# All experts' weights resident on chip, one VectorE copy per tile, states and layer norm in place, and a reordered step, in a fused attention and mixture-of-experts kernel

## The reference

```python
xn = _layernorm(x, axis=-1)
x = x + attn(xn) + ffn(xn)

# attn: per token, 8 heads of 16 channels
qkv = query @ W_qkv.T + b_qkv
qq, kq, vq = encode(q), encode(k), encode(v)     # unit length, times exp(1j*phase)
q_ent, k_ent = _entangle(qq, g), _entangle(kq, g) # DEPTH = 3 rounds over neighbouring heads
for c in range(CIRCUITS):                        # 4
    pattern = einsum('bsid,bsjd->bsij', conj(qa), ka)
    scores = abs(pattern) ** 2 * SCALING
    amps = sqrt(softmax(scores) + 1e-12)
    ...                                          # weighted values, clipped amplitude, mixed
return measured @ W_out.T + b_out

# ffn: top 2 of 8 experts, hidden size 512
topk_scores, topk_idx = top_k(x_flat @ Wg, 2)
h = gelu(x_flat @ W1[e] + b1[e]); out_e = h @ W2[e] + b2[e]
y = y + cw[:, e:e + 1] * out_e
```

## Time and profile before

| | |
|---|---|
| median of 3 runs | 1484.06 us (1478.45 to 1485.84) |
| the profiled execution, its own time | 1484.62 us |
| its span, first to last instruction | 1482.9 us |
| granted TensorE clock, mean | 0.813 of full speed |
| busy: PE, PEld | 947.4 us (64%), 750.0 us (51%) |
| busy: ACT, DVE, POOL | 740.2, 578.7, 431.4 us |
| DMA | 210.90 MB, 142 GB/s |

### The profile page before, as it was taken

How to read it: one execution, slowest core, us unless ns; L and a number is a source line. 1 busy time by engine, 2 the same in 40 slices (tenths; PEclk the granted TensorE clock), 3 DMA queues, 4 the chain that set the end, 5 groups by cost and what they waited for, 6 DMA issues and landing times.

```text
span 1482.9 us, 28381 instructions
## 1 busy us (share of the span) xinstructions
PE 947.4 (64%) x10529; PEld 750.0 (51%) x10529; DVE 578.7 (39%) x1098; ACT 740.2 (50%) x1602; POOL 431.4 (29%) x389
## 2 busy tenths in 40 slices
PE   3454748487583866858486594848658574866842
PEld 2324547375462746656364464637446463746531
DVE  5541615345160443437152252525425151433421
ACT  3422637365361755727373472836445282655522
POOL 3064101035022130707132040424603021251146
PEclk9865979889796897968798797878978787987965
DMA  7326474755847566695855758485674838576462
GB/s 216 103 82 150 124 148 118 148 158 160 152 135 126 135 146 143 170 173 147 159 133 129 145 149 151 126 178 145 161 159 133 145 106 178 147 151 153 132 103 71
DMA packets 320744, 210.90 MB, mean 142 GB/s; under 512 B 155296, under 2 KB 281952, under 8 KB 320096
## 3 DMA queue, kind: packets, MB, share of 16 engines
q1 hardware_dynamic: 311392, 188.10, 55.9%
q0 software_dynamic: 8192, 16.79, 3.8%
q10 hardware_dynamic: 1024, 4.20, 1.8%
HBM read 147.51 MB, written 61.50 MB: 141 GB/s over the span
## 4 chain that ended last, share of the span: by engine, by line
PE 42%; issue 26%; ACT 17%; POOL 5%; DVE 3%; SPq 3%; DMA 2%; ACTq 1%; POOLq 0%; DVEq 0%
PE ps_h L677 11%; PE ps_f L685 8%; PE ps_a L755 6%; PE ps_r L834 6%; PE ps_k L743 3%; POOL rows_in L1280 3%; ACT hid L1107 2%; PE ps_a L781 2%; ACT L1107 2%; ACT expo L1075 1%; ACT xy L1023 1%; PE ps_f L669 1%; PE ps_f L687 1%; ACT L1075 1%; ACT xy L1045 1%
## 5 line engine op out<-in xcount | busy, mean ns | idle before, releaser
L677 PE MATMUL ps_h<-turned,w_tile 128*128 128x128 f32 x1248 | 216.0, 328 | 334.0 <-issue 235.3
L677 PEld LDWEIGHTS ps_h<-turned,w_tile 128*128 128x128 f32 x1248 | 190.5, 231 | 371.4 <-issue 266.2
L1107 ACT ACTIVATE hid<-ps_h,w_tile 128x128 f32<-128x128 f32 x624 | 178.2, 368 | 340.5 <-PE ps_h L677 336.5
L685 PE MATMUL ps_f<-w_tile,hid 128*128 128x128 f32 x1248 | 198.7, 312 | 0.7 <-ACT turned L1100 0.7
L685 PEld LDWEIGHTS ps_f<-w_tile,hid 128*128 128x128 f32 x1248 | 187.0, 229 | 1.5 <-issue 1.0
L1252 POOL TENSOR_TENSOR sqx<-sqx,sqy 128x512 f32<-128x512 f32 x64 | 82.0, 1303 | 344.4 <-ACT sqy L1031 255.6
L1280 POOL DMA_INDIRECT rows_in<-xn,row_of x128 | 128.3, 1003 | 183.2 <-DVE tile_expert L1637 146.9
L1252 POOL TENSOR_TENSOR v_tok<-qkv,rnorm 128x512 f32<-128x512 f32 x16 | 41.4, 2587 | 395.3 <-DVE rnorm L1533 341.0
L834 PE MATMUL ps_r<-sqx,mats 128*128 128x512 f32 x256 | 132.6, 642 | 17.8 <-POOL sqx L1252 9.6
L1295 POOL DMA_INDIRECT got<-rows_out,row_of x112 | 109.1, 974 | 102.1 <-DMA rows_out<-turned 70.3
L755 PE MATMUL ps_a<-k_rows,q_rows 128*32 128x16 f32 x4096 | 102.2, 245 | 41.6 <-DMA k_rows<-states 29.0
(11 more groups left out here) (249 smaller groups left out, 1566.5 us busy)
## 6 DMA issues: line engine op xcount, KB each, us to landing
w_tile<-w_cat SPq DMA_DIRECT2D x156, 514.0 KB
states<-fxyT SPq DMA_DIRECT2D x32, 512.0 KB, 2.9
k_rows<-states SPq DMA_DIRECT2D x128, 128.0 KB, 5.4
x_tile<-rows_in SPq DMA_DIRECT2D x156, 64.0 KB, 3.1
rows_out<-turned SPq DMA_DIRECT2D x156, 64.0 KB
q_rows<-states SPq DMA_DIRECT2D x128, 64.0 KB, 5.1
rows_in<-v_rows SPq DMA_DIRECT2D x2, 2496.0 KB, 12.0
v_dram<-v_tok SPq DMA_DIRECT2D x16, 256.0 KB, 4.0
```

The source lines that it names most:

```text
L677: last = nc.tensor.matmul(ps_h[:, c, :], w_tile[:, n % WS, c * P:(c + 1) * P], turned[:, x_turn(n) % FS, 0, :], start=True, stop=True)
L685: nc.tensor.matmul(ps_f[:, 1, :], hid[:, n % 2, c, :], w_tile[:, n % WS, HID + c * C:HID + (c + 1) * C], start=(c == 0), stop=False)
L1107: act.activation(hid[:, n % 2, c, :], ps_h[:, c, :], ACT.Gelu, bias=w_tile[:, n % WS, HID + HC * C + c:HID + HC * C + c + 1]).then_inc(hid ...
```

## The change

**Weights.** All eight experts stay on chip: `w_res` holds, per expert, W1 (512 columns), b1 (4) and W2 (512), and `b2_res` the bias b2. `w_cat`, `w_tile`, `b_tile` and `load_weights` are gone. VectorE copies W1 and b1 of a tile's expert (516 columns) from `w_res` to one of three slots of `w_up` (`copy_ups`), and reads the expert into a register first; `tile_up` takes the weights from there. `tile_down` reads W2 and b2 straight from `w_res` and `b2_res` at an address in a register, so TensorE too reads `tile_expert` into a register for every tile.

**Room for that.** The states are grown in place in `xy1` (`fxyT` is gone); the layer norm is done in place in `xn` (`x_sb` is gone), so x is loaded a step later; `sqp`, `mixed`, `power` and `below` lie in `w_rows` and `u`; `got` has one buffer instead of two, so `gather` waits for the sum of the block before (`added_step` of `at - 1`).

**Order.** `pattern(k)` moves from the start of the step to behind the second tile, `grow_once`, `turn_w`, `weighted`, `mix_circuits` and the pieces of ScalarE and VectorE that belong to them move too; on SyncE `load_values`, `store_states` and `load_states` stand at three places instead of two.

```diff
@@ sync @@
-                if exists(ln_block(k + 1)):
-                    load_x(ln_block(k + 1))
+                if exists(ln_block(k)):
+                    load_x(ln_block(k))
...
-                    if at == 6 and exists(n_next):
-                        store_states(n_next)
                     if at == 7 and exists(n_next):
                         load_values(n_next)
-                    if at == 7 and exists(n_next):
+                    if at == 8 and exists(n_next):
+                        store_states(n_next)
+                    if at == 9 and exists(n_next):
                         load_states(n_next)
...
-                    if at == 10 and exists(k):
+                    if at == 11 and exists(k):
                         load_mixed(k)
...
-                    if n + WS < NTILES:
-                        load_weights(n + WS)
@@ tensor @@
-                pe.wait_ge(w_landed.of(n), w_landed.value(n))
+                pe.wait_ge(up_copied.sem, up_copied.value(n))
...
             def tile_down(n):
+                g, s = n // TILES, n % TILES
...
+                e = pe.value_load(tile_expert[0:1, g % GS, s:s + 1], min_val=0, max_val=E - 1)
                 pe.wait_ge(hidden_ready.sem, hidden_ready.value(n))
                 pe.wait_ge(turn_copied.sem, turn_copied.value(y_turn(n) - 1))
                 for c in range(HC):
-                    nc.tensor.matmul(ps_f[:, 1, :], hid[:, n % 2, c, :], w_tile[:, n % WS, HID + c * C:HID + (c + 1) * C],
-                                     start=(c == 0), stop=False)
+                    w2 = w_res[:, bass.ds(e, 1), UP + c * C:UP + (c + 1) * C].rearrange("p e n -> p (e n)")
+                    nc.tensor.matmul(ps_f[:, 1, :], hid[:, n % 2, c, :], w2, start=(c == 0), stop=False)
@@ gpsimd @@
-                elif at >= 2:
-                    pool.wait_ge(added_step.sem, added_step.value(at - 2))
+                elif at >= 1:
+                    pool.wait_ge(added_step.sem, added_step.value(at - 1))
...
-                for b in combined_at.get(k, []):
-                    add_rows(b)
+                for m, b in enumerate(waiting):
+                    if m >= 1:
+                        gather(b)
+                    if b in combined:
+                        add_rows(b)
@@ vector, new @@
+            def copy_ups(k, first, last):
+
+                for n in step_tiles.get(k, [])[first:last]:
+                    for m in ((0, 1, 2) if n == 0 else (n + 2,)):
...
+                        e = dve.value_load(tile_expert[0:1, g % GS, s:s + 1], min_val=0, max_val=E - 1)
+                        if m >= WS:
+                            dve.wait_ge(hidden_ready.sem, hidden_ready.value(m - WS))
+                        dve.tensor_copy(w_up[:, m % WS, :], w_res[:, bass.ds(e, 1), 0:UP].rearrange("p e c -> p (e c)")
+                                        ).then_inc(up_copied.sem, 1)
```

More of the change, by code:

```diff
@@ L244, in build @@
         u = sb("u", [P, 2, 4 * P])
+        power, below = (u[:, 0, n * 2 * P:(n + 1) * 2 * P].rearrange("p (n j) -> p n j", j=NH) for n in range(2))
         signed = [u, expo.rearrange("p c n -> p (c n)").rearrange("p (h n) -> p h n", h=2)]
         sup_mat = sb("sup_mat", [P, 2 * HD])
-        mixed = sb("mixed", [P, 4 * P])
-        scratch = [k_rows.rearrange("p r n -> p (r n)"), fxyT.rearrange("p a g c -> p (a g c)"),
+        scratch = [k_rows.rearrange("p r n -> p (r n)"), xy1.rearrange("p a g c -> p (a g c)"),
                    expo.rearrange("p c n -> p (c n)")]
@@ L432, in got_at @@
             if at < NB - 2:
-                return got[:, at % 2]
-            first = (NB - 6) % XN if at == NB - 2 else (NB - 4) % XN
-            return xnT[:, first:first + 2, :].rearrange("p s (t c) -> p s t c", t=T)
+                return got[:]
+            first = 2 * (at - (NB - 2))
+            return xn[:, first:first + 2]
         def mat(name):
@@ L629, in _ @@
                     s = n % TILES
-                    if n == 0:
-                        for m in range(WS):
-                            load_weights(m)
                     if s == 0:
@@ L676, in tile_up @@
                 for c in range(HC):
-                    last = nc.tensor.matmul(ps_h[:, c, :], w_tile[:, n % WS, c * P:(c + 1) * P],
+                    last = nc.tensor.matmul(ps_h[:, c, :], w_up[:, n % WS, c * P:(c + 1) * P],
                                             turned[:, x_turn(n) % FS, 0, :], start=True, stop=True)
@@ L889, in _ @@
                     target_tiles(n)
+                if exists(k):
+                    pattern(k)
                 if exists(o):
@@ L1074, in score_exp @@
                 for c in range(NC):
-                    act.activation(expo[:, c, :], below.rearrange("p n j -> p (n j)"), ACT.Exp,
+                    act.activation(expo[:, c, :], u[:, 0, 2 * P:4 * P], ACT.Exp,
                                    scale=gain[:, c:c + 1]).then_inc(exp_ready.sem, 1)
@@ L1173, in _ @@
                     control0(n)
+                tiles(k, 1, 2)
                 if exists(k):
-                    score_exp(k)
-                tiles(k, 1, 2)
+                    square_pattern(k)
                 if exists(o):
                     copy_mT(o)
-                tiles(k, 2, 3)
                 if exists(n) and exists(k):
@@ L1183, in _ @@
                     pass_first(n)
-                if exists(j):
-                    layer_norm(j)
                 if exists(k):
-                    amplitude(k)
+                    score_exp(k)
+                tiles(k, 2, 3)
                 if exists(o):
@@ L1320, in _ @@
                 o, n = k - 1, k + 1
-                for b in gathered_at.get(k, [])[0:1]:
-                    gather(b)
+                combined = combined_at.get(k, [])
+                waiting = gathered_at.get(k, [])
+                if waiting:
+                    gather(waiting[0])
                 scatter_part(k, 0)
@@ L1327, in _ @@
                     sum_squares(n, sq1_ready, sum1_ready)
-                for b in gathered_at.get(k, [])[1:3]:
-                    gather(b)
                 scatter_part(k, 1)
@@ L1333, in _ @@
                 scatter_part(k, 2)
-                for b in combined_at.get(k, []):
-                    add_rows(b)
+                for m, b in enumerate(waiting):
[3 more added lines that the diff above has]
+                        add_rows(b)
+                for b in combined:
+                    if b not in waiting:
+                        add_rows(b)
                 scatter_part(k, 3)
-                for b in gathered_at.get(k, [])[3:]:
-                    gather(b)
         @block.vector
@@ L1723, in _ @@
                     norm_squares(n)
+                if routed is not None:
+                    route(routed)
+                copy_ups(k, 0, 1)
+                if exists(n) and exists(k):
+                    normalise(n)
+                copy_ups(k, 1, 2)
+                if exists(o):
+                    measure(o)
                 if exists(j):
```

258 lines of the change are left out of this document (125 added, 133 removed).

## The result

The changed kernel takes **1544.28 us** in the median (1537.77 to 1548.94), the kernel before 1483.05 us beside it. The ratio is 1.0413, with a 95% interval of 1.0365 to 1.046: the change makes the kernel 4% slower, where 1412 us and 5% faster were predicted. The profiled execution's span is 1541.3 us.

A forecast was written before the change was run, and what follows sets the result against it. It took PE's wait for tile weights, behind the states' DMAs in SP's queue at 14 step boundaries, as the bound. 1484.6 - 248 + 70 + 20 + 23 + 42 + 6 + 15 gave 1412 us, range 1315 to 1490.

The forecast's parts named there:

- the +20 us for the inner order: Inside each step, moved pieces keep their lengths but more stand in one chain: +20 us, bounds -75 to +75.
- Rival 4: VectorE's copies come late, locked out of a shared SBUF port by GpSimd: 1448 us, chance 0.10.
- -248 us for the weights: At 14 step boundaries, TensorE's wait of 17.7 us for tile weights goes with weights on chip: -248 us.
- Rival 3: At the boundary the wait only changes its name, as the states land late: 1468 to 1483 us, chance 0.08.
- the 224 records of `pattern`: In `pattern`, 224 of 256 products take 5.45 us, read as 24 ns per product pair; +6 us at the start.
- The boundary: Between steps, TensorE waits for `a0` before `control_tiles`, 5.8 or 3.7 us, 5 in the mean: +70 us.
- The combining steps: In steps 5, 9 and 13, the single gather buffer makes ScalarE stand 13.6 us: 3 x 14 = +42 us.
- The tail: Behind the last tile, three further blocks take 16 us each, 48 us instead of 33: +15 us.
- Register work: On TensorE, reading the expert's number shows 0.1 to 0.2 us a tile: +23 us, bounds 0 and 226.
- Rival 2: Register work isn't hidden on TensorE, each tile pays 1.45 us: 1525 us, chance 0.12.

The follow-up runs named there:

- e7: The changed kernel with the turned states written into xy2 (onto the addend) instead of over x1 and y1: 1469.03 us, ratio 0.9932.
- e5: The changed kernel with an unused tensor of 128 bytes per partition declared early, so q_rows and k_rows start at multiples of 512 again: 1496.02 us, ratio 1.0126.
- e6: The kernel before with an unused tensor of 384 bytes per partition behind b1_cols, so q_rows and k_rows start 384 over a multiple of 512: 1528.06 us, ratio 1.0345.
- e1: The kernel before with 153 of the 156 pairs of weight loads left out, results wrong: 1357.04 us, ratio 0.9177.
- e9: The changed kernel in its own order, with the turned states in xy2 and the 128 unused bytes: 1426.09 us, ratio 0.9617.
- e2: The changed kernel with every tile using expert 0, no register loads and 3 copies instead of 156, results wrong: 1538.88 us, ratio 1.0385.
- e8: The changed kernel with the order of before, turned states in xy2, 128 unused bytes, and ScalarE's second and third weightings 2 and 4 tiles later: 1415.45 us, ratio 0.9577.
- e4: The changed kernel with, on SP alone, the store of mixed ahead of the states' loads and its loads right behind these: 1538.84 us, ratio 1.0401.

## Why the prediction was wrong, point by point

The steps where it failed first.

- **A part of the change was never priced: the states in place.** The sum has terms for weights, order, registers, copies, buffer and tail, and none for the states in place, though the title names them. The sentence "the moved pieces keep their lengths", on which the +20 us for the inner order rest, is where it slipped through. The turn kept neither its length (1.28 to 2.30 us) nor its start (4.23 us of wait a block): +75 us (e7). The diff did show it: the added wait on `sq2_ready` stands in `turned_states`, and the question "who waits for the same signal" would have led to GpSimd's `sum_squares`.
- **Rival 4 had the right mechanism on the wrong operation.** I asked whether the copies collide with GpSimd. They can, but they hardly meet: only 3 of the 156 overlap an addition of GpSimd. Two of them started first and took 0.42 us; the third started 0.06 us behind GpSimd and took 1.50 us, where the mean is 445 ns (VectorE, then GpSimd):

```profile
1246.10 1.50 DVE L1706 COPY w_up<-w_res 128x516 f32 x1
```

```profile
1246.04 2.67 POOL L1231 TENSOR_TENSOR yacc<-yacc,got 128x512 f32<-128x512 f32 x2 [5.52 <-ACT got L1108]
```

What meets GpSimd in every block is the turn, which reads two tensors from SBUF. The Trainium skill ("SBUF — State Buffer", SBUF: two separate sides) names this case too, a VectorE operation with two SBUF inputs against a GpSimd operation that reads SBUF, and calls it a lock for the whole instruction. The rows agree: the four operations end one behind the other, 4.55 us from the first start (879.13) to the last end, and side by side they would take 2.6. The operation of 3.078 us that I took for rival 4 stands beside two of GpSimd's sums as well (from 695.38 on in before).
- **A tensor that vanished moved its neighbours.** +48 us (e5, e6). No row of before could show this; only the addresses could.
- **-248 us for the weights was twice too large.** They were worth 122 us (e1, in the old order). I looked for what is next at the boundary only with `pattern` out of the way, and took it to be `a0`. Rival 3 (the wait only changes its name to `k_rows`) had a chance of 0.08 and was half right in the old order: the states' transfer was almost as late as the weights, for the same reason, SP's queue. In the new order PE waits elsewhere: with both faults out (e9) 23.0 us for `k_rows`, but 81.7 us for GpSimd's `sum_squares` before the growing products, 9.6 in the kernel before. No term of the sum has that wait.
- **That e9 measures 1426 us, 14 us over the forecast, is in part luck.** It is the change without the two faults, but errors of both signs cancel in it: too much for the weights and nothing for that last wait on one side, too much for the register work and the boundary on the other.
- *A slip without effect:* the 224 records of `pattern` are single matmuls, two to a product. So 24 ns is the time of one and 49 ns that of a product, and they are 224 of 256 matmuls.

The steps that held, by the trace of after:

```profile
752.68 1.54 PE L805 MATMUL ps_r<-ident,a 128*128 128x128 f32 x6 [4.97 <-DVE a L1457]
994.90 1.44 PE L655 MATMUL ps_h<-turned,w_up 128*128 128x128 f32 x5 [20.53 <-ACT turned L1078]
1524.73 1.11 PE L785 MATMUL ps_t<-ident,meas 128*128 128x128 f32 x4 [30.09 <-DVE meas L1457]
```

- *The boundary*: 5.0 us before `control_tiles` where 5.8 were worked out, and 2.2 to 2.5 where 3.7 were; in all 47.7 us in 12 waits, where the sum has 70. The mechanism is right, the size a third too large.
- *The combining steps*: ScalarE stands 13.7 to 13.8 us before the second weighting of steps 5, 9 and 13, where 13.6 were worked out, and PE's wait there is 19.7 to 20.5 us instead of the 3.1 to 4.3 of other steps, some 16 more, where 14 were predicted.
- *The tail*: from the start of the last tile's up (1402.47 and 1440.39) to the end of the span, 80 us before and 101 us after. +20 instead of +15, and the last wait in it is for `measure`, not for a gather.
- *Register work*: 23 us were taken, 5 or none were found (e2). TensorE's sequencer does run ahead: PE stands 3.1 us in all before the products of `tile_down`. Rival 2 is out.

The old order's numbers close as well. e8 is 0.0400 of before, 59 us, slower than e1, which has the order and no resident weights; their profiled spans differ by 61.3 us. From the start of one `pattern` to the start of the next, the three combining steps (5, 9 and 13) are 29.6 us longer in e8, the twelve others 14.4 us together, and from the last `pattern` to the end it is 16.2 us; 1.1 us lie ahead of the first. So the resident weights' machinery is about 1.2 us a step, and what is left to mend lies where rows are gathered.

What stays open: why the wait at `measure` could shrink by 41 us for nothing (e4), that is, which other chain holds the step of after there; what PE's 81.7 us behind GpSimd's sums in the new order cost, and whether the pieces can be placed so that they go; and whether most of the 59 us could be had with a second gather buffer (not tried; it takes 4096 more bytes of each partition).

## What to carry to other kernels

When a result is written over its input, list every other reader of that input: the writer now waits for the last of them, and starts together with everything else that this last reader releases. When a tensor is added or removed, compare the start addresses of the tiles that DMAs read and write in short rows (512 bytes here) modulo 256 bytes before reasoning about anything else, and pad where they moved. Before a large wait is taken off in full, find what the same queue issues right behind it; a run with only that wait gone (e1) costs little and shows what the wait was covering.

## What the hardware showed unexpectedly

- 128 unused bytes per partition make 3% of this kernel, in both directions, through rows of 512 bytes that start 128 bytes off (landing in 5.0 to 5.4 us against 6.8 to 7.1). The one bad start that was run is 384 over a multiple of 512.
- VectorE's 128 x 1024 scalar_tensor_tensor from SBUF takes 1.28 us alone and 2.30 us beside GpSimd's 128 x 512 sums, whose pair grows from 2.49 to 3.47 us. Started together, the four end in turns, 1.08 to 1.13 us apart, in all 16 blocks.
- A register load on TensorE takes 0.302 us in the median (0.304 on VectorE), less than the 0.462 us on SP, and 156 of them on each engine, with the copies, cost 5 us or nothing (e2):

```profile
L665 PEldq TENSOR_LOAD <-tile_expert x156: 296/302/905, 139.0 to 1441.0; - x156
```
